# Loading synthesis tap tables and half of the first image while the strips still run, in a Swin-style filter-bank kernel

## The reference, cut to what matters

```python
B, C, H, W = (8, 16, 56, 56); K = 9; FS = 9; DIM = K * C + C      # 160 features
x2 = relu(x)
sub = conv(x2, f_ana)                          # 9 filters of 9x9 on each channel
x3 = concatenate([sub, x2]).transpose(...)     # tokens of 160 features
for i, (shift, mask) in enumerate(zip(SHIFTS, (None, MASK1))):
    x3 = _swin_block(x3, shift, mask, ...)     # window attention and MLP, twice
y = (x3 @ linw + linb).transpose(0, 3, 1, 2)   # 144 channels: 9 filters x 16
ti = y.reshape(B, K, C, H, W).transpose(0, 2, 1, 3, 4).reshape(B * C, K, H, W)
y_trans = conv(ti, f_syn).reshape(B, C, H, W)  # 9x9 synthesis, sums over the 9 filters
out = conv1x1(concatenate([y_trans, y]), convw) + convb
```

## Time and profile before

| | |
|---|---|
| median of 3 runs | 3139.16 us (3137.38 to 3139.48) |
| the profiled execution | 3129.97 us |
| its span, first to last instruction | 3128.2 us |
| mean granted TensorE clock | 0.984 of full speed |
| TensorE matmuls busy | 2986.7 us, 95% of the span |
| VectorE busy | 2224.6 us, 71% |
| ScalarE busy | 1714.9 us, 55% |
| GpSimd busy | 841.0 us, 27% |
| data moved | 147.28 MB, mean 47 GB/s |

### The profile page before, as it was taken

How to read it: one execution, slowest core, us unless ns; L and a number is a source line. 1 busy time by engine, 2 the same in 40 slices (tenths; PEclk the granted TensorE clock), 3 DMA queues, 4 the chain that set the end, 5 groups by cost and what they waited for, 6 DMA issues and landing times. The chain is left out here.

```text
span 3128.2 us, 102845 instructions
## 1 busy us (share of the span) xinstructions
PE 2986.7 (95%) x39898; PEld 2694.2 (86%) x39898; DVE 2224.6 (71%) x6742; ACT 1714.9 (55%) x4076; POOL 841.0 (27%) x1464
## 2 busy tenths in 40 slices
PE   7959999999999999999999999999999999999589
PEld 5759888889888888888888988898888888888589
DVE  4667777777777777777777777777777777777322
ACT  5436666656655666666555555555555655565221
POOL 8112222222222222222232233223322233222110
PEclk9979999999999999999999999999999999999899
DMA  6321111111111111112111111111111111111484
GB/s 143 117 85 29 37 39 39 39 39 39 39 32 38 39 33 31 39 39 59 43 35 32 32 39 39 32 27 39 39 33 26 39 39 33 26 39 27 81 146 83
DMA packets 210423, 147.28 MB, mean 47 GB/s; under 512 B 15954, under 2 KB 205205, under 8 KB 210331
## 3 DMA queue, kind: packets, MB, share of 16 engines
q1 hardware_dynamic: 208627, 145.85, 19.9%
q0 software_dynamic: 1728, 0.48, 0.2%
HBM read 95.64 MB, written 52.50 MB: 47 GB/s over the span
## 5 line engine op out<-in xcount | busy, mean ns | idle before, releaser
L1490 PE MATMUL rm<-w,ht 128*112 128x160 f32 x4480 | 681.0, 301 | 0.0
L1490 PEld LDWEIGHTS rm<-w,ht 128*112 128x112 f32 x4480 | 610.0, 177 | 5.4 <-ACT ht L1067 0.2
L977 POOL TENSOR_TENSOR rs<-ln_tmp,mhalf 112x4 f32<-112x4 f32 (+1 forms) x128 | 119.3, 932 | 1620.0 <-DVE ln_tmp L1149 1619.9
L1067 ACT ACTIVATE ht<-rm 128x448 f32<-128x448 f32 (+1 forms) x640 | 319.2, 499 | 190.7 <-PE rm L122 190.7
L1032 ACT ACTIVATE vb<-ra 113x320 f32<-113x320 f32 x256 | 113.1, 442 | 278.4 <-PE ra L122 276.8
L122 PE MATMUL rm<-z2t_hi,w_hi 128*128 128x448 f32 (+1 forms) x640 | 256.9, 401 | 4.6 <-DVE z2t_rest L1259 3.5
L943 POOL TENSOR_TENSOR z<-z,one 112x448 f32<-112x448 f32 (+2 forms) x192 | 131.6, 685 | 346.6 <-DVE z L1153 346.6
L122 PE MATMUL rm<-z2t_rest,w_rest 98*128 98x448 f32 (+1 forms) x640 | 219.0, 342 | 0.0
L122 PE MATMUL rm<-z2t_lo,w_hi 128*128 128x448 f32 (+1 forms) x640 | 218.5, 341 | 0.0
L122 PE MATMUL rm<-z2t_hi,w_lo 128*128 128x448 f32 (+1 forms) x640 | 217.1, 339 | 0.0
L1198 DVE TENSOR_TENSOR sc<-so,tabs 113x490 f32<-113x490 f32 x256 | 171.2, 669 | 58.8 <-PE so L1436 46.4
(11 more groups left out here) (253 smaller groups left out, 8861.9 us busy)
## 6 DMA issues: line engine op xcount, KB each, us to landing
xa<-xs SPq DMA_DIRECT2D x128, 245.0 KB
xr<-xs SPq DMA_DIRECT2D x128, 245.0 KB
xs<-xo SPq DMA_DIRECT2D x64, 245.0 KB
ys<-yz SPq DMA_DIRECT2D x64, 245.0 KB
c_y<-ys SPq DMA_DIRECT2D x48, 260.0 KB
xs<-a_tok SPq DMA_DIRECT2D x14, 560.0 KB, 6.5
xs<-tok_late SPq DMA_DIRECT2D x14, 560.0 KB, 6.9
c_y<-ys SPq DMA_DIRECT2D x16, 280.0 KB
```

The source lines that it names most:

```text
L977: gp.tensor_tensor(rs[1][:, t0:t0 + nt], ln_tmp[1][5][:, t0:t0 + nt], mhalf[:, 0:nt], ALU.pow).then_inc(s_pow, 1)
L1067: act_(ht[:, f * SN + t0 * TT:f * SN + (t0 + nt) * TT], bank_m(i, lm, use)[:, 0:nt * TT], ACT.Gelu_apprx_tanh).then_inc(m_freed(i, lm, use ...
L1490: last = mm(bank_m(i, lm, use)[0:TT, t * DIM:(t + 1) * DIM], ht[:, c:c + TT], keep.w["w2", lm][:, f * DIM:(f + 1) * DIM], start=(f == 0), ...
```

## The change

`LastPair` becomes `Handed`, and `tok_late` stays allocated through phase C. Into it go, in phase B, tap pieces 0 to 4 (5040 floats per partition), and the first half of image 0 behind them (2240 floats, 7280 of 7840 in all). The 20 tap transfers are issued by SyncE just before `body(NS - 2)`, behind the wait for the margins; the five of the half image just before `body(2 * NS - 2)`. In phase C only piece 5 and the second half of image 0 are loaded for the start, then image 1. Piece 0 is made ahead of the first half on ScalarE and VectorE, and ScalarE waits for each half of image 0 by itself. The first half of the even images lies in `tok_late` from then on.

```diff
+class Handed:
+    def __init__(self, nc, ctx, xs0, ys, f_syn):
+        self.s_taps = ctx.enter_context(nc.semaphore("taps_early"))
+        self.s_y = ctx.enter_context(nc.semaphore("c_y_in0"))
...
+    def load_taps(self, sp, n, t, off, s_taps):
+        h, j = divmod(n, CJ)
+        for ro in range(RB):
+            a0 = RB * j - ro + RB - 1
+            sp.dma_start(view(t, 0, 128, off + ro * TB, [[1, TB]]),
+                         dram(self.f_syn.tensor, (h * TA + a0) * XW * TB, [[TB, 128], [1, TB]])).then_inc(s_taps, 16)
+    def load_half(self, sp, img, h, t, off, s_y):
...
 (phase B, SyncE)
             repeat_margins(0, B - 1)
             sp.wait_ge(s_dup, 48 * (B - 1))
+            for n in range(TAPS_EARLY):
+                late.load_taps(sp, n, late.tok, n * PIECE, late.s_taps)
             body(NS - 2, 0, 0, 1)
...
             with sp.Fori(NS + 1, 2 * NS - 2) as i:
                 body(i, 1, 1, 1)
+            sp.wait_ge(s_yz, 64 * SPI)
+            late.load_half(sp, 0, 0, late.tok, Y_EARLY, late.s_y)
             body(2 * NS - 2, 1, 1)
             body(2 * NS - 1, 1, 1)
             body(2 * NS, None, 1)
             sp.wait_ge(s_yz, 64 * NS)
+            sp.wait_ge(late.s_taps, 16 * RB * TAPS_EARLY)
+            sp.wait_ge(late.s_y, HALF_IN)
...
 (phase C, SyncE)
-            load_image(0, 0)
-            for n in range(G * J):
-                load_taps(n)
-                if n == J - 1:
-                    load_image(1, 1)
+            load_image(0, 0, (1,))
+            for n in range(TAPS_EARLY, G * J):
+                late.load_taps(sp, n, taps_last, 0, s_taps)
+            load_image(1, 1)
...
 (phase C, ScalarE)
-                    if h == 0:
+                    if first(img):
+                        act.wait_ge(s_y[u], (h + 1) * HALF_IN)
+                    elif h == 0:
                         act.wait_ge(s_y[u], (pair + 1) * Y_IN)
...
+                    if h == 0 and first(img):
+                        band(0)
                     nc.scalar.activation(view(y_hi, 0, 128, (h * YB + 1) * KC, split),
-                                         view(y[u], 0, 128, h * NB4 * DIM, whole), ACT.Copy).then_inc(s_hi, 1)
+                                         view(y[u][h][0], 0, 128, y[u][h][1], whole), ACT.Copy).then_inc(s_hi, 1)
                     if first(img):
-                        for n in range(h * J, (h + 1) * J):
+                        for n in range(max(h * J, 1), (h + 1) * J):
                             band(n)
```

More of the change, by code:

```diff
@@ L72 @@
 TA = 2 * RB + FS - 2
+CJ = 3
+PIECE = RB * TB
+TAPS_EARLY = 5
+Y_EARLY = TAPS_EARLY * PIECE
+HALF_IN = 16 * (RB + 1)
 def view(t, p0, n, off, dims):
@@ L133, in build @@
         keep = Persistent(nc, ctx)
[L134 to L139, removed]
+        late = Handed(nc, ctx, xs0, ys, f_syn)
+        phase_a(nc, keep, late, x, f_ana, ln1g, ln1b, qkvw, qkvb, projw, projb, rel, relT, ln2g, ln2b, w1, b1,
+                w2, b2, linwT, linb, convwT, convb, wmask, xs0)
+        phase_b(nc, keep, late, xs0, xs1, ys)
+        phase_c(nc, keep, late, out)
 class Persistent:
@@ L164, in split @@
         return (sb(name + "_hi", [128, n], F32R), sb(name + "_lo", [128, n], F32R), sb(name + "_rest", [CK, n], F32R))
-class LastPair:
-    def __init__(self, nc, ctx, xs0):
-        self.xs0 = xs0
+class Handed:
+    def __init__(self, nc, ctx, xs0, ys, f_syn):
+        self.xs0, self.ys, self.f_syn = xs0, ys, f_syn
         self.tok = ctx.enter_context(nc.sbuf_tensor("tok_late", [128, WT * DIM], F32))
         self.s_store = ctx.enter_context(nc.semaphore("store_late"))
+        self.s_taps = ctx.enter_context(nc.semaphore("taps_early"))
+        self.s_y = ctx.enter_context(nc.semaphore("c_y_in0"))
     def store_pair(self, sp, pair, tok, s_store):
@@ L180, in store_pair, with taps @@
                          view(tok, 0, 128, oy * WIN * DIM, [[1, WIN * DIM]])).then_inc(s_store, 16)
+    def taps(self, n):
+        return view(self.tok, 0, 128, n * PIECE, [[XO, K], [TB, RB], [1, XO]])
+    def load_taps(self, sp, n, t, off, s_taps):
[5 more added lines that the diff above has]
+    def load_half(self, sp, img, h, t, off, s_y):
+        base = img * (H * YW * DIM)
+        x0 = h * (W - XW) * DIM
+        for r in range(RB):
+            b0 = 0 if r == RB - 1 else 1
+            row = RB * b0 + r - SHIFT
+            sp.dma_start(view(t, r * XW, XW, off + b0 * DIM, [[DIM, NB4 - b0], [1, DIM]]),
+                         dram(self.ys, base + row * YW * DIM + x0, [[DIM, XW], [RB * YW * DIM, NB4 - b0], [1, DIM]])
+                         ).then_inc(s_y, 16)
+        sp.dma_start(view(t, 0, SHIFT * XW, off, [[1, DIM]]),
+                     dram(self.ys, base + (H - SHIFT) * YW * DIM + x0, [[YW * DIM, SHIFT], [DIM, XW], [1, DIM]])
+                     ).then_inc(s_y, 16)
 def phase_a(nc, keep, late, x, f_ana, ln1g, ln1b, qkvw, qkvb, projw, projb, rel, relT, ln2g, ln2b, w1, b1, w2, b2,
@@ L1608, in _, with phase_c @@
             bodies(pe, body)
-def phase_c(nc, keep, f_syn, ys, out):
+def phase_c(nc, keep, late, out):
     with ExitStack() as ctx:
@@ L1617, in sem @@
             return ctx.enter_context(nc.semaphore(name))
-        G, J = 2, 3
+        G, J = 2, CJ
         KC = K * C
@@ L1622, in phase_c @@
         YB = NB4 + 2
-        PIECE = RB * TB
         acc = [ctx.enter_context(nc.psum_tensor(f"c_acc{n}", [128, 512], F32)) for n in range(2)]
         fin = [ctx.enter_context(nc.psum_tensor(f"c_fin{n}", [128, 512], F32)) for n in range(2)]
-        taps = [sb(f"c_taps{n}", [128, PIECE]) for n in range(2)]
+        taps_last = sb("c_taps", [128, PIECE])
         band_hi = sb("c_band_hi", [128, G * J * PIECE], F32R)
         band_lo = sb("c_band_lo", [128, G * J * PIECE], F32R)
-        y = [sb(f"c_y{u}", [128, G * NB4 * DIM]) for u in range(2)]
+        HALF_Y = NB4 * DIM
+        y_rest = [sb("c_y0", [128, HALF_Y]), sb("c_y1", [128, G * HALF_Y])]
+        y = [[(late.tok, Y_EARLY), (y_rest[0], 0)], [(y_rest[1], 0), (y_rest[1], HALF_Y)]]
         y_hi = sb("c_y_hi", [128, G * YB * KC], F32R)
@@ L1636, in phase_c @@
         res = [sb(f"c_res{u}", [NP, G * 2 * NP]) for u in range(2)]
-        s_taps = [sem(f"c_taps_in{n}") for n in range(2)]
+        s_taps = sem("c_taps_in")
         s_bhi, s_blo, s_zero, s_sel = sem("c_band_hi_done"), sem("c_band_lo_done"), sem("c_zero"), sem("c_sel_set")
-        s_y = [sem(f"c_y_in{u}") for u in range(2)]
+        s_y = [late.s_y, sem("c_y_in1")]
         s_hi, s_lo = sem("c_y_hi_done"), sem("c_y_lo_done")
@@ L1644, in phase_c, with taps @@
         s_store = [sem(f"c_store{u}") for u in range(2)]
-        Y_IN = 16 * 2 * (RB + 1)
+        Y_IN = 2 * HALF_IN
         def first(img):
             return isinstance(img, int) and img == 0
+        def taps(n):
+            return late.taps(n) if n < TAPS_EARLY else view(taps_last, 0, 128, 0, [[XO, K], [TB, RB], [1, XO]])
         def y_dims():
@@ L1656, in _, with load_image @@
         def _(sp):
[L1657 to L1681, removed]
-            load_image(0, 0)
-            for n in range(G * J):
-                load_taps(n)
-                if n == J - 1:
-                    load_image(1, 1)
+            def load_image(img, u, halves=(0, 1)):
+                for h in halves:
+                    late.load_half(sp, img, h, *y[u][h], s_y[u])
+            load_image(0, 0, (1,))
+            for n in range(TAPS_EARLY, G * J):
+                late.load_taps(sp, n, taps_last, 0, s_taps)
+            load_image(1, 1)
             def store_image(img, u):
@@ L1728, in body @@
                         ins = gp.tensor_tensor(view(direct[u], 0, 128, h * NC, [[NB4, C], [1, NB4]]),
-                                               view(y[u], 0, 128, h * NB4 * DIM + KC, [[1, C], [DIM, NB4]]),
+                                               view(y[u][h][0], 0, 128, y[u][h][1] + KC, [[1, C], [DIM, NB4]]),
                                                view(one, 0, 128, 0, [[0, C], [0, NB4]]), ALU.mult)
@@ L1739, in band @@
             def band(n):
-                act.wait_ge(s_taps[n % 2], 16 * RB * (n // 2 + 1))
-                nc.scalar.activation(view(band_hi, 0, 128, n * PIECE, [[NP, K], [XO, RB], [1, XO]]),
-                                     view(taps[n % 2], 0, 128, 0, [[XO, K], [TB, RB], [1, XO]]), ACT.Copy).then_inc(s_bhi, 1)
+                if n < TAPS_EARLY:
+                    act.wait_ge(late.s_taps, 16 * RB * TAPS_EARLY)
+                else:
+                    act.wait_ge(s_taps, 16 * RB)
+                nc.scalar.activation(view(band_hi, 0, 128, n * PIECE, [[NP, K], [XO, RB], [1, XO]]), taps(n),
+                                     ACT.Copy).then_inc(s_bhi, 1)
             def sum_out(img, u):
@@ L1785, in band @@
                 nc.vector.tensor_tensor(view(band_lo, 0, 128, n * PIECE, dims),
-                                        view(taps[n % 2], 0, 128, 0, [[XO, K], [TB, RB], [1, XO]]),
+                                        taps(n),
```

(6 more changed lines are left out.)

## The result

| | median of runs, us | range |
|---|---|---|
| before | 3138.27 | 3134.97 to 3139.48 |
| changed | 3113.72 | 3112.75 to 3120.16 |

The ratio is 0.9928, with a 95% interval from 0.9911 to 0.9945: faster by 17 to 28 us. The medians differ by 24.6 us, where 23.5 were forecast. The profiled execution of the changed kernel took 3113.33 us, with a span of 3111.5.

The account below looks back on a forecast made before the run. Until 2983.45 us, waits for image 0 and tap piece 3 in phase C bound the kernel, then TensorE. Gain 23.5 at phase C's start, minus 0 for phase B: 3139.16 - 23.5 = 3115.7 us; 8-in-10 range 3109 to 3122.

Parts of the forecast that it names:

- zero: Start of phase C: SyncE's first transfer in it, at 2940.13 us in the profile before.
- T: Phase C, start of image 0's `turned`: forecast to move from 3002.12 to 2978.6 us.
- the first 162 matmuls: Phase C start: first 81 take 10.57 us as before, the second 81 follow at once at full clock, ending 2965.8.
- the gap: Phase C, after 162 matmuls: TensorE stands 4.3 us (3.7 to 4.8) until image 1 is landed and rounded.
- 81 matmuls to T: Phase C, after the wait for image 1: 8.42 us at full clock before image 0's `turned`.
- What sets the end of the chain: Phase C: waits for transfers, last for image 1, set when `turned` starts; TensorE bounds what follows; gain 23.5 us.
- The start and the landings: Phase C: TensorE starts at 2946.85, half 1 lands at 2948.7, image 1 at 2965.8 us.
- no gap: Rival, phase C: image 1 comes by 2961.5, so TensorE doesn't wait; gain 27.8, 3111.3 us; chance 0.08.
- The clock after the gap: Phase C, after the wait for image 1: clock stays at full, chance 0.49; falling has 0.2 and costs 1.6 us.
- The gain: Start of phase C: 3002.12 - 2978.6 = 23.5 us, with nothing taken off for phase B.
- cold after the gap: Rival, phase C: clock falls during the wait for image 1, costing 1.6 us; gain 21.9, 3117.3 us; chance 0.2.
- Strip 30: Phase B: 20 tap issues take 9.4 us ahead of `xa`, hidden by 5 us of cover; cost taken as nothing.

Follow-up runs that it names:

- changed, second trace: The changed kernel run again with no edit, for a second trace: median 3113.05 us, ratio 0.9920 against the kernel before.
- the threefold loads: Changed kernel with the 20 early tap transfers issued three times at strip 30, waiting after the first two rounds: 3134.75 us, ratio 0.9991 against the kernel before.

## Why the prediction was right, and where it was off

The way from zero to T, in us (rounded, so that a sum can be off by 0.1):

| | forecast | changed | changed, second trace |
|---|---|---|---|
| to the first matmul | 6.7 | 6.6 | 6.6 |
| the first 162 matmuls | 19.0 | 19.8 | 18.8 |
| the gap | 4.3 | 3.2 | 3.9 |
| 81 matmuls to T | 8.4 | 10.0 | 10.8 |
| T | 38.5 | 39.6 | 40.0 |

- **What sets the end of the chain:** right. T moved by 22.0 us, the ratio gives 22.6, and the kernel is then the same to the end. The two halves of the change, done alone, moved T by 12.2 and 11.2 us (their ratios, 11.9 and 11.6).
- **The start and the landings:** right. Half 1 was forecast at 8.6, measured 8.8; image 1 at 25.7, measured 25.4 and 25.0 (the lower end of its range is 2965.4 by the terms given, not 2965.2). The rival *no gap* didn't happen. The mean rate doesn't set the landing: by the single microseconds some 4.8 MB had moved between zero and the landing of image 1, where image 1 and what stood ahead of it are 3.9. So about 1 MB of image 2 was in ahead of the last bytes of image 1, which fits some of the 16 DMA engines being behind the others, as the prediction has it; no run shows which. Whether image 1 lands earlier when image 2 is held back was not tried.
- **The first 162 matmuls:** forecast "as before", and it lies between the two traces. The clock's rise scatters by more than 2 us from one execution to the next, and each us of it makes these matmuls half a us longer.
- **The gap:** forecast 4.3 us. In the first trace it is shorter by the 0.8 us that the matmuls ahead of it took longer, and by 0.3 of landing. What starts late in front of a fixed landing is free.
- **The clock after the gap:** the term that was off. I gave the clock falling in the gap 0.2 and staying 0.49. It fell in both traces of the changed kernel, and the 81 matmuls took 10.0 and 10.8 us, 1.6 and 2.4 more. The row that I had (TensorE stopped at 2972.57, the clock fell in the microsecond from 2976) puts the fall 3.4 to 4.4 us after the stop, so a gap of 4.3 us was as long as that, and 0.2 was too little by my own row. That row was also one draw: worked out from the mean clocks of single microseconds, the fall came 2.0 to 4.9 us after TensorE stopped in the eight traces that have such a gap ahead of T, 3.4 and 2.2 in the two of the changed kernel. The Trainium skill (TensorE: Matmul & The Clock Gate, "HAM oscillation"), by which a wait for a transfer between groups of matmuls can leave the next group cold, had it right here: each of these eight gaps, 3.2 us the shortest, was followed by matmuls at the lower clock.
- **The gain:** the forecast took T before as 3002.12, 0.35 us behind the first matmul of `turned`. By the marks its gain was therefore 23.2 us, and 22.0 came, as in the rival *cold after the gap* (21.9). The medians moved by 24.6, in both timings of the changed kernel. The 2.6 us more than the marks show are within the intervals (17 to 28 us, and 19 to 31 for the second) and stay unexplained. That the medians' 24.6 is so near to 23.5 is in part luck.
- **Strip 30:** right. Issue took 9.39 us (9.4 forecast), and nothing waited. The cover was 5 us by the forecast and 5.2 by the threefold loads.
- **The level:** the profiled execution of before, at 3129.97 us, was 8 us under the median of its runs. Taking the gain off the median, not off the profile, was right: the level that scatters lies ahead of phase C.

What stays open is why the clock in the last strips, and its rise at the start of phase C, differ from one execution to the next. No experiment was aimed at it.

## What to carry to other kernels

A load that is moved early helps twice: by its own wait, and by the queue time that it frees for whatever is loaded behind it. Here the second set the end, so ask what lands last after the change, and add up the bytes ahead of it on the queue. A wait for a whole buffer where half is used first costs on top: here some 5 us, saved by one more semaphore for each buffer. When a moved transfer is free, work out how much room it has by the deadline of the next load behind it; here each us beyond that room cost about one. And before a difference of one or two us between two traces is put down to the kernels, look at a second trace of each.

## What was not expected of the hardware

After a gap of 3.2 us TensorE's clock was at the lower level for the next matmuls, though it read 1.00 to the end of the gap; after one of 1.3 us it wasn't. The rise after the first matmul of phase C took 3.6 to 6.1 us in ten traces, with 4.3 and 5.9 in two traces of the same kernel. Two executions of one kernel began phase C 4.0 us apart with 0.99 and 0.87 as the mean clock of a stretch of 40 us (2900 to 2940). About 1 MB of image 2 moved ahead of the last bytes of image 1, which was issued before it on the same queue.
